# Weights into the one-hots: summing incoming and outgoing edges of a graph layer on one core

## The reference

```python
h = (feat - mean) * rsqrt(var + EPS) * gamma + beta
feat_in = h @ W_in + b_in
feat_out = h @ W_out + b_out
a_in = segment_sum(feat_in[src] * iw[:, None], dst)
a_out = segment_sum(feat_out[dst] * ow[:, None], src)
xi = concatenate((a_in, a_out), axis=1) @ W_x2i + b_x2i
hh = h @ W_h2h
i_i, i_n = split(xi, 2, axis=1)
h_i, h_n = split(hh, 2, axis=1)
h = tanh(i_n + h_n) + sigmoid(i_i + h_i) * (h - tanh(i_n + h_n))
# then a layer norm of x + h, and a second layer: node features shifted and
# scaled by column, segment_sum over dst with the same weights, @ weight + bias
```

## Time and profile before

| | us |
|---|---|
| median of 3 runs | 3975.26 (3967.52 to 3986.59) |
| profiled execution | 3983.03 |
| its span in the profile | 3981.2 |
| busy: PE, DVE, ACT, POOL | 2656.6, 2302.5, 1059.2, 2607.6 |
| first gathers, scatter, second gathers | 448, 1254, 807 |
| gates, second layer | 202, 1233 |

### The profile page before, as it was taken

One profiled execution on the slowest core, in us unless ns is written; L12 is line 12 of the kernel. 1 busy time (PEld: TensorE's weight loads), 2 busy tenths in 40 slices (PEclk: granted clock), 3 DMA queues, 4 the chain that ended last, 5 costly groups with the idle time before them and its releaser, 6 DMA issues.

```text
span 3981.2 us, 47940 instructions
## 1 busy us (share of the span) xinstructions
PE 2656.6 (67%) x10701; PEld 1905.5 (48%) x10701; DVE 2302.5 (58%) x4510; ACT 1059.2 (27%) x3137; POOL 2607.6 (65%) x2706
## 2 busy tenths in 40 slices
PE   4666766566666566648888888996656545545467
PEld 4455543333333333337777777643434334333356
DVE  6866866566565565645666666686335445444355
ACT  3233322222222222224444444463000000000012
POOL 5666666666666666665666666476667777777764
PEclk8777777777787877779999999998777777777688
DMA  5443343333343333347878887554333333333333
GB/s 149 138 130 106 95 139 130 130 133 132 128 140 131 134 130 130 128 150 236 248 246 244 249 245 245 182 166 137 90 90 93 93 94 91 91 93 93 91 115 97
DMA packets 275042, 565.31 MB, mean 142 GB/s; under 512 B 55583, under 2 KB 121110, under 8 KB 274771
## 3 DMA queue, kind: packets, MB, share of 16 engines
q0 software_dynamic: 119808, 329.02, 26.5%
q1 hardware_dynamic: 146304, 223.88, 18.3%
q10 hardware_dynamic: 8660, 9.41, 0.7%
HBM read 419.19 MB, written 142.88 MB: 141 GB/s over the span
## 4 chain that ended last, share of the span: by engine, by line
PE 34%; another core or an unknown queue 26%; issue 17%; DVE 11%; POOL 7%; ACT 2%; DMA 1%; DVEq 1%; SPq 1%; ACTq 0%; POOLq 0%
PE ps L1140 10%; PE ps L952 8%; POOL messages L547 6%; PE ps L1211 5%; PE ps L1072 3%; PE ps L1101 2%; PE ps L1173 2%; PE ps L1258 1%; ACT arena L729 1%; DVE arena L1758 1%; POOL arena L541 1%; DVE ps L1582 1%; DVE arena L1761 1%; PE ps L1087 1%
## 5 line engine op out<-in xcount | busy, mean ns | idle before, releaser
L547 POOL DMA_INDIRECT messages<-arena x832 | 830.1, 998 | 428.8 <-issue 239.2
L541 POOL DMA_INDIRECT arena<-in_x,arena x832 | 792.7, 953 | 471.1 <-issue 209.2
L619 POOL DMA_INDIRECT arena<-x_table,wh x832 | 841.4, 1011 | 365.8 <-issue 241.8
L1211 PE MATMUL ps<-arena 128*128 x2048 | 597.0, 443 | 385.5 <-issue 134.7
L1211 PEld LDWEIGHTS ps<-arena 128*128 128x128 f32 x2048 | 438.1, 222 | 549.4 <-issue 487.3
L952 PE MATMUL ps<-arena 128*128 128x128 f32 x3328 | 490.5, 309 | 238.6 <-issue 168.4
L952 PEld LDWEIGHTS ps<-arena 128*128 128x128 f32 x3328 | 462.3, 221 | 319.6 <-issue 270.9
L729 ACT ACTIVATE arena<-ps,arena 128x256 f32<-128x256 f32 x832 | 325.1, 481 | 910.3 <-remote 435.0
L1072 PE MATMUL ps<-arena 128*128 128x256 f32 x1664 | 489.8, 447 | 10.7 <-issue 5.2
L2174 DVE TENSOR_TENSOR node_a<-node_a,ps 128x256 f32 x256 | 106.8, 417 | 637.3 <-remote 453.9
L1072 PEld LDWEIGHTS ps<-arena 128*128 128x128 f32 x1664 | 381.8, 231 | 104.2 <-issue 38.2
(11 more groups left out here) (280 smaller groups left out, 3374.9 us busy)
## 6 DMA issues: line engine op xcount, KB each, us to landing
arena<-messages SPq DMA_DIRECT2D x464, 260.0 KB
arena<-in_x SPq DMA_DIRECT2D x304, 128.0 KB, 2.9
gate_rows<-arena SPq DMA_DIRECT2D x49, 384.0 KB
arena<-gate_rows SPq DMA_DIRECT2D x49, 384.0 KB, 3.0
arena<-in_x,arena POOLq DMA_INDIRECT x832
messages<-arena POOLq DMA_INDIRECT x832
arena<-x_table,wh POOLq DMA_INDIRECT x832
arena<-in_x SPq DMA_DIRECT2D x48, 256.0 KB
```

The costliest lines, as they stand in the source:

```text
L541: nc.gpsimd.indirect_dma_start(out=big[:, s, j, 0:D], out_offset=None, in_=x, in_offset=bass.IndirectOffsetOnAxis(ap=ids[:, j:j + 1], axis ...
L547: nc.gpsimd.indirect_dma_start(out=messages, out_offset=bass.IndirectOffsetOnAxis(ap=ids[:, j:j + 1], axis=0), in_=big[:, s, j, :], in_off ...
L619: nc.gpsimd.indirect_dma_start(out=last_rows[:, (g + 1) % LAST_ROWS, j * D:(j + 1) * D], out_offset=None, in_=x1_table, in_offset=bass.Ind ...
L1211: last = nc.tensor.matmul(ps[g % LAST_SUMS][:, 0:D], last_hot[h][:, j, :], last_rows[:, bass.ds(k, 1), j * D:(j + 1) * D].rearrange("p o d ...
```

## The change

- Places are taken modulo 128. A one-hot then refers to positions in two neighbouring node tiles. `node_a` now has nodes on partitions, 256 features and one column for the sum of the weights (AW = 257). The product of a group is added twice by DVE, into the tile and the next one, each time multiplied by a mask of 0 and 1 per partition that says which part of the product belongs there (`low_mask`, `high_mask`).
- In `in_mm` the one-hots stand still and rows of 257 move: 4 products in place of 8 of 128 columns. Column 257 sums the weights, so that the separate sums during the scatter are gone, with their two one-hot passes, the reduction, the matmul and the additions.
- In the first gathers ACT copies the weights into column 257, one instruction a group more. In the second gathers ACT no longer scales rows; column 257 holds 1.0, and DVE multiplies the one-hots by the weights (`weigh=True`).
- At the start a few short operations on DVE make the masks and a packed table of tile numbers, fed by one broadcast DMA on SP behind a wait; two transposes on PE go. `node_c` is cleared in ten parts during the last ten turns of the scatter that have a tile, not partly between the scatter and the second gathers. The two DMAs of the weight row go.
- In the gates the incoming sums are turned as well: 4 transposes a tile in place of 2.

```diff
+AW = D + 1
...
+            sp.wait_ge(S["weights_turned"], 4)
+            sp.dma_start(lows_b, row_view(group_row).broadcast_to([P, NG])).then_inc(S["low_rows"], 16)
...
-            sp.wait_ge(S["w_summed"], 1)
-            sp.dma_start(row_view(weight_row), in_w_row[:, 0:NT * P]).then_inc(S["row_kept"], 16)
...
+                nc.scalar.activation(big[:, s, :, D:AW], carried[:, bass.ds((RING * i + s) * CPG, CPG), 1:2], ACT.Copy)
...
             act.wait_ge(S["back_cleared"], 1)
-            for g in range(RING * FIRST, NG_PLAIN):
-                in_scale(g // RING, g % RING)
-                for q in pairs_of(g):
-                    keep(q, q % RING)
-            with act.If(general):
-                with act.Fori(PLAIN, ALL) as i:
-                    scale_turn(i)
+            for q in range(PAIRS):
+                keep(q, q % RING)
...
-                    nc.scalar.activation(node_rows[:, s, :], tile_of(node_c, t), ACT.Copy).then_inc(S["e_rows"], 1)
+                    nc.scalar.activation(node_rows[:, s, 0:D], tile_of(node_a, t), ACT.Copy)
+                    nc.scalar.activation(node_rows[:, s, D:2 * D], tile_of(node_c, t), ACT.Copy).then_inc(S["e_rows"], 1)
                 if is_tile(t - 1):
                     need(act, S["e_mm"], t - 2)
-                    nc.scalar.activation(st[:, r, 0:2, :], in_sums[:, :, bass.ds((t - 1) * P, P)], ACT.Copy)
                     act.wait_ge(S["e_turned"], t)
-                    nc.scalar.activation(st[:, r, 2:4, :], halves(ps[r][:, 0:D]), ACT.Copy).then_inc(S["e_out"], 1)
+                    nc.scalar.activation(st[:, r, :, :], ps[r][:, :].rearrange("p (k n) -> p k n", k=4), ACT.Copy).then_inc(S["e_out"], 1)
...
+            def in_mm(i, s, scaled=True):
                 g, h = RING * i + s, s % 2
-                pe.wait_ge(S["in_scaled"], g + 1)
+                if scaled:
+                    pe.wait_ge(S["in_scaled"], g + 1)
+                else:
+                    pe.wait_ge(S[f"in_rows{s}"], (i + 1) * 16 * CPG)
                 pe.wait_ge(S["in_hot"], g + 1)
-                need(pe, S["in_added"], g - 1)
-                for k in range(2):
-                    for j in range(CPG):
-                        last = nc.tensor.matmul(ps[4 + h][:, k * P:(k + 1) * P], big[:, s, j, k * P:(k + 1) * P],
-                                                hot[:, h, j, :], start=j == 0, stop=j == CPG - 1)
+                need(pe, S["in_added"], 2 * (g - 1))
+                for j in range(CPG):
+                    last = nc.tensor.matmul(ps[4 + h][:, 0:AW], hot[:, h, j, :], big[:, s, j, 0:AW], start=j == 0, stop=j == CPG - 1)
                 last.then_inc(S["in_mm"], 1)
...
-                    if s % 2:
-                        pe.wait_ge(S["w_hot"], g + 1)
-                        need(pe, S["w_added"], g - 1)
-                        if s == 1 and tiles:
-                            pe.wait_ge(S["c_out"], i + 1)
-                        nc.tensor.matmul(ps[4][0:1, 0:2 * P], ones[:, 0:1], weighed.rearrange("p k n -> p (k n)"),
-                                         start=True, stop=True).then_inc(S["w_mm"], 2)
                     if s == 0 and tiles:
                         pe.wait_ge(S["cx_loaded"], (i + 1) * 16)
                         need(pe, S["c_out"], i)
-                        need(pe, S["w_added"], g)
...
-                    for k in range(2):
+                    for k in range(4):
                         last = nc.tensor.transpose(ps[s % 2][:, k * P:(k + 1) * P], node_rows[:, s % 2, k * P:(k + 1) * P], ident[:, :])
...
-            def hot_in(g, s, numbers):
+            def hot_in(g, s, numbers, weigh=False):
                 need(dve, S["in_mm"], g - 1)
-                V.tensor_tensor(hot[:, s % 2, :, :], numbers[:, :].rearrange("p (o n) -> p o n", o=1).broadcast_to([P, CPG, P]),
+                equal = V.tensor_tensor(hot[:, s % 2, :, :], numbers[:, :].rearrange("p (o n) -> p o n", o=1).broadcast_to([P, CPG, P]),
                                 place[:, bass.ds(g * CPG, CPG)].rearrange("p (c o) -> p c o", o=1).broadcast_to([P, CPG, P]),
-                                ALU.is_equal).then_inc(S["in_hot"], 1)
...
-            def add_in(g, s, low):
+                                ALU.is_equal)
+                if weigh:
+                    equal.then_inc(S["in_equal"], 1)
+                    dve.wait_ge(S["in_equal"], g - RING * FIRST + 1)
+                    V.tensor_tensor(hot[:, s % 2, :, :], hot[:, s % 2, :, :], carried[:, bass.ds(g * CPG, CPG), 1:2].broadcast_to([P, CPG, P]),
+                                    ALU.mult).then_inc(S["in_hot"], 1)
+                else:
+                    equal.then_inc(S["in_hot"], 1)
+            def windows(n, of, table, most=NT):
+                v = V.value_load(table[0:1, bass.ds(n, 1)]).with_bounds(min_val=0, max_val=1 << (4 * WIN_BITS))
+                return [((v >> (WIN_BITS * u)) & ((1 << WIN_BITS) - 1)).with_bounds(min_val=0, max_val=most) for u in of]
+            def low_tiles(i, of=range(RING)):
+                return windows(i, of, low_four, (N - P) // P)
+            def add_in(g, s, tile, kept=False):
                 dve.wait_ge(S["in_mm"], g + 1)
-                need(dve, S["in_added"], g)
-                o = in_sums[:, :, bass.ds(low, P)]
-                V.tensor_tensor(o, o, halves(ps[4 + s % 2][:, 0:D]), ALU.add).then_inc(S["in_added"], 1)
-            def in_turn(i, beside=(), first=False, last=False, between=None, numbers=numbers_in):
+                need(dve, S["in_added"], 2 * g)
+                for k, mask_of in ((0, low_mask), (1, high_mask)):
+                    m = carried[:, bass.ds(g, 1), 2 + k] if kept else mask_of[:, bass.ds(g, 1)]
+                    o = tile_of(node_a, tile + k, AW)
+                    V.scalar_tensor_tensor(o, ps[4 + s % 2][:, 0:AW], m, o, ALU.mult, ALU.add).then_inc(S["in_added"], 1)
...
+            fours, shifted_tile = (low_four[:, k * (NG // RING):(k + 1) * (NG // RING)] for k in range(2))
+            link(V.tensor_scalar(fours, lows[:, :, 0], 7, None, ALU.logical_shift_right))
+            for u in range(1, RING):
+                link(V.tensor_scalar(shifted_tile, lows[:, :, u], 7, WIN_BITS * u, ALU.logical_shift_right, ALU.logical_shift_left))
+                link(V.tensor_tensor(fours, fours, shifted_tile, ALU.bitwise_or))
             dve.wait_ge(S["constants"], 5)
+            dve.wait_ge(S["low_rows"], 16)
+            link(V.tensor_scalar(lows_b, lows_b, P - 1, None, ALU.bitwise_and))
+            link(V.tensor_copy(splits, lows_b))
+            V.tensor_scalar(low_mask, splits, pcol[:, :], None, ALU.is_le)
+            link(V.tensor_scalar(high_mask, splits, pcol[:, :], None, ALU.is_gt))
             dve.wait_ge(S["sums_cleared"], 2)
...
-            def add_weights(i, s):
-                g = RING * i + s
-                lows = two_lows(i, s)
-                dve.wait_ge(S["w_mm"], g + 2)
-                for k in range(2):
-                    need(dve, S["w_added"], g + k)
-                    o = in_w_row[:, bass.ds(lows[k], P)]
-                    V.tensor_tensor(o, o, ps[4][0:1, k * P:(k + 1) * P], ALU.add).then_inc(S["w_added"], 1)
-            def out_hots(i, s, numbers=numbers_out, hots=None):
+            def out_hots(i, s, hots=None):
                 g, h = RING * i + s, s % 2
                 dve.wait_ge(S["places_spread"], g + 1)
                 spread = ps[5] if hots is None else ps[6]
                 V.tensor_scalar(hot_flat(h) if hots is None else hots, spread[:, :], pcol[:, :], None, ALU.is_equal).then_inc(S["out_hot"], 1)
-                need(dve, S["w_hot"], g - 1)
-                V.tensor_tensor(hot_w[:, h, :, :], numbers.rearrange("p (o n) -> p o n", o=1).broadcast_to([P, CPG, P]),
-                                place[:, bass.ds(g * CPG, CPG)].rearrange("p (c o) -> p c o", o=1).broadcast_to([P, CPG, P]),
-                                ALU.is_equal).then_inc(S["w_chain"], 1)
+            def carry(i, s):
+                g = RING * i + s
                 need(dve, S[f"sent{s}"], i * 16 * CPG)
-                carry = V.tensor_copy(big[:, s, :, D:D + RW], carried[:, bass.ds(g * CPG, CPG), :])
+                last = V.tensor_copy(big[:, s, :, D:D + RW], carried[:, bass.ds(g * CPG, CPG), :])
                 if staged_turn(i):
-                    carry = V.tensor_copy(stage[:, s, :], slot[:, bass.ds(g * CPG, CPG)])
-                carry.then_inc(S["out_carried"], 1)
-                dve.wait_ge(S["w_chain"], 2 * g + 1)
-                V.tensor_tensor(hot_w[:, h, :, :], hot_w[:, h, :, :], carried[:, bass.ds(g * CPG, CPG), 1:2].broadcast_to([P, CPG, P]),
-                                ALU.mult).then_inc(S["w_chain"], 1)
-                dve.wait_ge(S["w_chain"], 2 * g + 2)
-                need(dve, S["w_mm"], g - 1)
-                V.tensor_reduce(weighed[:, h, :], hot_w[:, h, :, :].rearrange("p j n -> p n j"), AX.X, ALU.add).then_inc(S["w_hot"], 1)
```

(32 more changed lines are left out.)

185 lines of the change are left out of this document (81 added, 104 removed).

## The result

The changed kernel takes 4013.22 us (median of 8 runs, 3998.13 to 4022.87) against 3975.16 us (8 runs, 3966.64 to 3986.59): a ratio of 1.0096 with a 95% interval of 1.0080 to 1.0113. That is 38 us slower, 26 us above the forecast of 3987 and inside the range.

The account below looks back on a forecast made before the run. It took POOL's scatters and stalls to bound the scatter, and POOL's gathers plus a late in_mm signal the second gathers. +2 +3 -50 -1 +50 +8 = +12 gave 3995.0 profiled, 3987 median; range 3860 to 4085.

Parts of the forecast that it names:

- Second gathers, forecast +50: Second gathers: 41 us from two-pair groups plus 9 for groups without margin, bounds 0 to 154 us.
- the old period taken as a floor: Second gathers: POOL's 4.7 us plus 1.4 set the 6.11 us period; one-pair groups stay at 6.1, two-pair reach 6.5.
- The rival of the full loop: Second gathers: DVE is in the loop, every group lengthens by 1.2 us, 154 in place of 50, 4091 us; chance 0.14.
- That all hides: Second gathers: the added 1.2 us fit into gaps, 0 in place of 50, 3937 us; chance 0.08.
- Scatter, forecast -50: Scatter: 25 us from scatters no longer lengthened and 25 from fewer stalls, between 0 and -209 us.
- The half for the lengthened scatters: Scatter: without L1771, which lengthens scatters issued beside it, 25 us go, bounds 0 and 29.
- The half for the stalls: Scatter: PE reaches its messages earlier, so POOL stalls less; 25 us taken, bounds 0 and 180.5.
- That the scatter is freed: Scatter: DVE and PE's mutual waits vanish, all but 15 of the stalls' 180 us go, -190, 3847 us; chance 0.22.
- Gates, +8 forecast: Gates: two more transposes a tile cost 0.1 to 0.5 us, 5 to 25 over 49 tiles; +8 taken.
- First gathers: Stretch to the first scatter: +2 us at the start and +3 for the second additions, mostly hidden in DVE's idle time.
- Layer two: Second layer: nothing in it changes, 0 us.
- The product against POOL's gathers: Second gathers: the two-SBUF-operand product could lengthen POOL's gathers, at most 51 us, behind DVE in two-pair groups.

Follow-up runs that it names:

- e1: Changed kernel with ScalarE scaling the rows again in the second gathers, no weight product on DVE: 3514.07 us against 3506.88 for the kernel before, 1.0018.
- e3: Changed kernel without the second addition in the second gathers: that stage takes 708.3 us against 751.1 in the changed kernel.
- e10: Kernel before, scatter's weighted one-hot made by four operations with places in PSUM: 3482.84 us against 3503.70, 0.9941, on a chip with prompt signals.
- e11: Same kernel as e10, on chip 1, the one with late signals: 3994.38 us against 3976.32 for the kernel before, 1.0049.
- b0: Kernel before, unedited, profiled on chip 2 as the base for the stages: 3510 us for the one profiled run.
- e4: Changed kernel plus a useless DVE product per scatter group, both operands in SBUF: scatter takes 1070.5 us against 1060.2 in the changed kernel.
- e5: As e4, but one operand of the added product in PSUM: scatter takes 1064.8 us against 1060.2 in the changed kernel.
- e8: Changed kernel without first gathers' second addition and two gate transposes: first scatter at 432.2 us against 438.9, last addition to layer two 205.4 against 214.2.

## Why the prediction was right, and where not

**Second gathers, forecast +50, measured +45.1.** The prices of DVE's two additional operations (0.47 and 0.7 us) were those forecast. On the chips with prompt signals the cause is shown by e1 and e3: 60 and 43 of 75 us come back when one of the two operations goes. On the chip of the measurement no edit of the changed kernel ran; there the cause is read from the waits. The step of the prediction that failed is the old period taken as a floor, a loop of POOL's four gathers and 1.4 us behind them under every group, so that one-pair groups would stay at 6.1 us and two-pair groups go to 6.5. One-pair groups fell to 4.7 us, and two-pair groups split into 5.4 to 6.1 us, under the old period, and 7.3 to 9.4 us, behind runs of 8 gathers; their mean is 6.85. The two errors cancel to 5 us. They seem not to be independent, since the runs of 8 gathers lie beside the short groups, but the prediction had neither, and that its number came so close is luck. On the chips with prompt signals PE's own 5.26 us a group was the bound before, and the loss was 75 us. The rival of the full loop (4.9 us from start to signal, 154 us more) is refuted by the same 4.7 us groups, and on chip 2, where nothing waits for a late signal, the wait behind the modelled end is absent for the same matmuls. That all hides is refuted too.

**Scatter, forecast -50, measured -23.3.** The half for the lengthened scatters was right: the mean went from 998 to 961 ns, 30 us, and L1771 alone stands beside 25.5 us of the excess before, where I had put 25. e10 and e11 show the cause: they keep the sums and nearly all of DVE's work (2302 us busy in e10, 2306 in b0), and with no second SBUF operand in the product the mean falls to 961 and 964 ns. e4 and e5 agree in direction. The Trainium skill, "SBUF — State Buffer", section "SBUF: two separate sides", says that a DVE operation with two SBUF inputs and a GpSimd operation that reads SBUF lock each other out of a shared pair of ports. The traces agree with this: with one operand in PSUM none of the 88 scatters beside the product was longer. The half for the stalls was the mis-sized term: I put 25 us for fewer waits, and the waits stayed. Over the whole stage POOL waited 180.8 us in 49 times for ACT and 14.9 in 10 for DVE, against 187.5 in 47 and 2.1 in 7. PE and DVE were freed from each other and it gained nothing. DVE's one-hots (L1749) instead stood 511 us for late signals of PE, so I read it that a late signal comes when POOL stops, whenever PE was done; no run tests this. That the scatter is freed is refuted on this chip; on chip 2 there was nothing to free, since POOL waited under 33 us before and after. e11 shows the reverse: with shorter scatters and the same sums the waits took more than the scatters gave. So the gain of a shorter scatter on such a chip is not sure even in sign; why the waits of e11 grew and those of the change hardly did stays open.

**Gates, +8 forecast, +11.0 measured.** By the starts of DVE's L2005 (L1970 after) a tile takes 3.86 us instead of 3.70, which is the 0.16 that was forecast; the other 3 us lie ahead of the first tile. e8 gives 8.8 of the 10.0 us of its chip to the two transposes.

**First gathers.** -1.2 for +5. The second addition does cost 7 us on a chip with prompt signals (e8); on chip 2 POOL waits 11.5 us for PE instead of 3.6. Beside late signals it hid: DVE's idle time ahead of its additions fell from 115 to 74 us, and POOL's wait for PE stayed, 61 us for 63.

**Layer two.** +8.1 for 0. I can't put this down to the change: e11, which changes nothing there, shows +8.8, and on chip 2 the change shows -8.3. I take it for spread between profiles. It is a part of the 26 us by which the forecast was low; the scatter's missing 27 is the larger one.

**The product against POOL's gathers.** It was bounded at 51 us. Gathers have a median of 946 ns (949 before), and a longest of 1456 instead of 962; the mean in the second gathers is 960 instead of 948, 6 us in 495. By the start times 31 gathers are over 0.04 us longer than the median, and 30 of them started while the product L1499 ran. Whether these 6 us lengthen the stage was not tested.

## What to carry to other kernels

Before adding work to an engine with little idle time per step, ask whether what it waits for is a law or an accident: the idle time ahead of the addition was 1.2 us a group on one chip and 0.1 on another. Here some steps of the loop became shorter and others longer; the mean period hides this, and the single periods show it. Price a freed engine only by what the bound engine waited for. An operation with two SBUF operands on DVE made two thirds of the scatters that started beside it in the kernel before longer, by 0.27 us on average (37 of 95, by 0.18 us, in e4). Taking one operand from PSUM avoids it, and of all edits here that one alone beat the kernel before, on a chip where the signals are prompt.
